# Between two layers of a graph and mixture-of-experts stack: row statistics, turning and head products tile by tile, residual products postponed, maxima two heads ahead instead of three

## What is computed

```
x = x + graph_conv(layernorm(x))                 # layer 0
x = x + attention_and_experts(layernorm(x))      # layer 0, 8 experts, 2 per row, and a shared one
x = x + graph_attention(layernorm(x))            # layer 1, 12 heads of 64   <- the change is in front of it and in it
x = x + experts(layernorm(x))                    # layer 1, 8 experts, 2 per row
```

```
ft = hh @ W_fc.T ;  a1 = ft . attn_l ;  a2 = ft . attn_r
e = leaky_relu(a1[src] + a2[dst], 0.2) ;  m = segment_max(e, dst)
alpha = exp(e - m[dst]) / segment_sum(...)
out = relu(hh @ W_res.T + segment_sum(alpha * ft[src]))
```

## Time and profile before

| | |
|---|---|
| time, median of 3 runs | 1669.37 us (1667.52 to 1672.15) |
| the profiled execution | 1672.59 us, of which the span of the trace is 1670.9 us |
| TensorE busy | 1500.3 us (90%) |
| VectorE busy | 1276.2 us (76%) |
| ScalarE busy | 854.8 us (51%) |
| GpSimd busy | 332.7 us (20%) |
| mean granted TensorE clock | 0.941 of full speed |

### The profile page before, as it was taken

One profiled execution on the slowest core, in us unless ns is written; L12 is line 12 of the kernel. 1 busy time (PEld: TensorE's weight loads), 2 busy tenths in 40 slices (PEclk: granted clock), 3 DMA queues, 4 the chain that ended last, 5 costly groups with the idle time before them and its releaser, 6 DMA issues. The chain is left out here.

```text
span 1670.9 us, 36622 instructions
## 1 busy us (share of the span) xinstructions
PE 1500.3 (90%) x14493; PEld 1277.6 (76%) x14493; DVE 1276.2 (76%) x2205; ACT 854.8 (51%) x1215; POOL 332.7 (20%) x254
## 2 busy tenths in 40 slices
PE   7987877887899999999999669966899999999997
PEld 5664445665567899999998534436899999999995
DVE  8998376775566688888888578857788888888786
ACT  1112116775544567777675125444566666666651
POOL 0004004655030000000004036655330000000040
PEclk9998898999899999999999769886999999999999
DMA  7640000000465678888886001113978888888884
GB/s 202 157 107 0 0 1 10 1 1 17 164 206 178 234 271 291 307 301 295 299 298 194 1 24 31 32 53 106 358 254 294 290 300 293 293 300 287 294 271 109
DMA packets 55554, 297.59 MB, mean 178 GB/s; under 512 B 14063, under 2 KB 14319, under 8 KB 32433
## 3 DMA queue, kind: packets, MB, share of 16 engines
q1 hardware_dynamic: 41761, 263.23, 46.0%
q0 software_dynamic: 13712, 33.26, 7.3%
HBM read 264.07 MB, written 32.34 MB: 177 GB/s over the span
## 5 line engine op out<-in xcount | busy, mean ns | idle before, releaser
L717 PE MATMUL ps<-big,wh 128*128 128x176 f16 x2160 | 497.4, 240 | 5.5 <-DVE wl L572 3.5
L721 PE MATMUL ps<-big,wl 128*128 128x176 f16 x2160 | 497.5, 239 | 0.0
L719 PE MATMUL ps<-big,wh 128*128 128x176 f16 x2160 | 497.4, 239 | 0.0
L738 PE MATMUL ps<-big,wh 128*128 128x176 f16 x2160 | 263.8, 239 | 3.0 <-DVE big L606 2.9
L738 PE MATMUL ps<-big,wl 128*128 128x176 f16 x1080 | 249.6, 240 | 0.0
L572 DVE SCALAR_TENSOR_TENSOR wl<-ext,wh 128x2304 f16<-128x2304 f32 x90 | 229.6, 2551 | 1.1 <-issue 0.9
L572 DVE SCALAR_TENSOR_TENSOR wl<-raw,wh 128x2304 f16<-128x2304 f32 x90 | 229.5, 2550 | 0.0
L493 ACT ACTIVATE wh<-raw 128x2304 f16<-128x2304 f32 x90 | 190.4, 2117 | 62.7 <-PE ps L738 51.6
L493 ACT ACTIVATE wh<-ext 128x2304 f16<-128x2304 f32 x90 | 190.5, 2117 | 51.3 <-PE ps L738 35.4
L717 PEld LDWEIGHTS ps<-big,wh 128*128 128x128 f16 x2160 | 209.2, 97 | 9.1 <-issue 3.4
L719 PEld LDWEIGHTS ps<-big,wh 128*128 128x128 f16 x2160 | 211.7, 98 | 0.2
(11 more groups left out here) (345 smaller groups left out, 2837.8 us busy)
## 6 DMA issues: line engine op xcount, KB each, us to landing
raw<-in_units SPq DMA_DIRECT2D x54, 1152.0 KB, 5.3
ext<-in_units SPq DMA_DIRECT2D x54, 1152.0 KB, 5.6
raw<-in_units SPq DMA_DIRECT2D x36, 1153.0 KB, 5.9
ext<-in_units SPq DMA_DIRECT2D x36, 1153.0 KB, 6.3
raw<-in_units_s SPq DMA_DIRECT2D x16, 769.0 KB, 4.5
ext<-in_units_s SPq DMA_DIRECT2D x16, 769.0 KB, 4.6
x_slots<-raw SPq DMA_DIRECT2D x1, 8976.0 KB
big<-x_slots POOLq DMA_DIRECT2D x17, 528.0 KB, 8.5
```

The lines of the kernel that those rows point to most:

```text
L717: nc.tensor.matmul(o, wh[:, u % RING, w_], x_, start=c == 0 and m == 0, stop=False, skip_group_check=True)
L719: nc.tensor.matmul(o, wh[:, u % RING, w_], xTl[:, c, 0:ph.n], start=False, stop=False, skip_group_check=True)
L721: ins = nc.tensor.matmul(o, wl[:, u % RING, w_], x_, start=False, stop=c == KC - 1, skip_group_check=True)
L738: ins = nc.tensor.matmul(o, l_[:, u % RING, w_], r_, start=first and k == 0 and c % 2 == 0, stop=last and k == 2, skip_group_check=True)
```

## The change

- The fence between the layers goes. VectorE's statistics are made tile by tile between the last adds: statistics of tiles 0 and 1, last add of tile 2, statistics of 2, last add of 3, statistics of 3, one square root for tiles 0 to 3 (on ScalarE ahead of the copies that fold the head weights), last add of 4, normalisation of 0 to 3; then statistics, root and normalisation of tile 4.
- TensorE turns tile by tile (6 blocks of one tile into banks 2, 3 or 0, 1), ScalarE alone copies the turned tiles to SBUF, and TensorE makes the head products of a tile (`head_values`, 6 of 132 columns, banks 4 to 7, each waiting for its tile's copy) in alternation with the turning of later tiles.
- The residual products are made apart, one tile at a time in banks 4 and 5 (`residual`, 6 of 128 columns, each waiting for the copy of the one before), among the steps of heads 0 and 1; ScalarE copies them in between.
- The maxima run two heads ahead instead of three: two heads before the loop, head h+2 in iteration h.
- `shifts_transposed(h+2)` moves in TensorE's stream from behind chunk 4 of head h-1 to between chunks 2 and 3 of head h. `shift_out(h+2)` moves in ScalarE's stream from behind exp 0 to behind exp 3, ahead of `head_out(h-1)`.
- In the last pass of layer 1's experts `gathered(1, 1)` is done one unit earlier. Copies of a1 and a2 are one instruction instead of two. The small work on gates and branches comes after a1's copy.

```diff
@@ scalar
-            fence(act, F_LAYER0)
-            root()
-            transposed_out()
+            root_part(4, NT)
             for t in range(NT):
-                act.wait_ge(s_ft, t + 1)
-                at = (4 * (t % 2) + 2) * BANK
-                nc.scalar.activation(z[:, t, :], ps[0:P, at:at + D], ACT.Copy).then_inc(s_fta, 1)
+                act.wait_ge(s_zT, t + 1)
+                nc.scalar.activation(tD[:, :, t * P:(t + 1) * P], z_turned(t), ACT.Copy).then_inc(s_zTa, 1)
+            def residual_out(t):
+                act.wait_ge(s_res, t + 1)
+                nc.scalar.activation(z[:, t, :], bank(4, 2)[0:P, 0:D], ACT.Copy).then_inc(s_fta, 1)
...
+            residual_out(0)
+            residual_out(1)
             shift_out(0)
+            residual_out(2)
+            residual_out(3)
             shift_out(1)
+            residual_out(4)
             for h in range(H):
                 for t in range(NT):
                     edge_exp(h, t)
-                    if t == 0:
-                        if h:
-                            sums_out(h - 1)
-                        if h + 2 < H:
-                            shift_out(h + 2)
+                    if t == 0 and h:
+                        sums_out(h - 1)
+                    if t == 3 and h + 2 < H:
+                        shift_out(h + 2)
                     if t == 3 and h:
                         head_out(h - 1)
@@ vector
+            dve.wait_ge(s_add, 2)
+            row_stats(0)
+            row_stats(1)
+            last_added(0, 2)
+            dve.wait_ge(s_add, 3)
+            row_stats(2)
+            last_added(0, 3)
+            dve.wait_ge(s_add, 4)
+            step(row_stats(3))
+            roots_asked(0, 4)
+            last_added(0, 4)
+            roots_of(0, 4)
             dve.wait_ge(s_add, NT)
-            fence(dve, F_LAYER0)
-            layernorm()
...
+            step(row_stats(4))
+            roots_asked(4, NT)
+            roots_of(4, NT)
...
-            for h in range(3):
+            for h in range(2):
                 for t in range(NT):
                     edge_top(h, t)
                 shifts(h)
             for h in range(H):
                 for t in range(NT):
                     edge_power(h, t)
-                if h + 3 < H:
+                if h + 2 < H:
                     for t in range(NT):
-                        edge_top(h + 3, t)
+                        edge_top(h + 2, t)
                         if t == 1 and h:
                             sums_inverted(h - 1)
-                    shifts(h + 3)
+                    shifts(h + 2)
@@ tensor
+            def z_transposed(t):
+                pe.wait_ge(s_zt, t + 1)
+                if t == 1:
+                    pe.wait_ge(s_add, NT)
                 if t >= 2:
+                    pe.wait_ge(s_zTa, t - 1)
+                for c in range(KC):
+                    ins = nc.tensor.transpose(z_turned(t)[:, c, :], z[:, t, c * 128:(c + 1) * 128], ident[0:P, 0:P])
+                ins.then_inc(s_zT, 1)
...
+            z_transposed(0)
+            z_transposed(1)
+            pe.wait_ge(s_fold, 6)
+            for t in range(NT):
+                head_values(t)
+                if t + 2 < NT:
+                    z_transposed(t + 2)
...
+            pe.wait_ge(s_a12, 1)
             source_row(0)
+            residual(0)
+            residual(1)
             shifts_transposed(0)
             source_row(1)
             flat_rows(0)
+            residual(2)
+            residual(3)
             shifts_transposed(1)
-            source_row(2)
+            residual(4)
+            pe.wait_ge(s_fta, NT)
             for h in range(H):
-                if h + 3 < H:
-                    source_row(h + 3)
+                if h + 2 < H:
+                    source_row(h + 2)
                 if h:
                     head_chunk(h - 1, 4)
-                if h + 2 < H:
-                    shifts_transposed(h + 2)
-                if h:
                     head_back(h - 1)
                 head_chunk(h, 0)
                 if h + 1 < H:
                     flat_rows(h + 1)
                 for t in range(1, 4):
                     head_chunk(h, t)
+                    if t == 2 and h + 2 < H:
+                        shifts_transposed(h + 2)
```

More of the change, by code:

```diff
@@ L46 @@
 C_ZERO, C_ALL = 2, 14
-F_GRAPH, F_MHA, F_LAYER0 = range(1, 4)
-R_Z0, R_HS, R_Z1 = range(1, 4)
+F_GRAPH, F_MHA = range(1, 3)
+R_Z0, R_HS = range(1, 3)
 def f16_pair(v):
@@ L609, in vector_steps, with ffn_vector @@
             return low, x_low, hidden
-        def ffn_vector(dve, ph, steps, at_last, step):
+        def ffn_vector(dve, ph, steps, at_last, step, adds):
             low, x_low, hidden = steps
             layer = 0 if ph is ph_0 else 1
-            sums = layer * 2 * NT
+            gathered, last_added = adds
             def one_pass(i, last):
@@ L632, in one_pass @@
                         gathered(layer, 0)
+                    if u == ph.ic - 2 and last and layer == 1:
+                        gathered(layer, 1)
                 dve.wait_ge(ph.down, ph.base + (i + 1) * ph.ic + RING)
@@ L659, in placed_last @@
                     ins.then_inc(s_lastpl, 1)
[L661 to L678, removed]
             with dve.Fori(0, at_last) as i:
@@ L682, in ffn_vector @@
             one_pass(at_last, True)
-            gathered(layer, 1)
+            if layer == 0:
+                gathered(layer, 1)
             dve.wait_ge(ph.yt, at_last * 3 + 5)
@@ L1306, in root_of @@
                 step(nc.vector.tensor_tensor(dst_, dst_, rs[:, 2, :], ALU.mult))
[L1308 to L1314, removed]
-                    ins = nc.vector.bn_aggr(mv[:, t, :], st[:, t, 0:2, :].rearrange("p a b -> p (a b)"))
-                step(ins)
-                nc.vector.tensor_scalar(rs[:, 0, :], mv[:, :, 1], 1e-5, None, ALU.add).then_inc(s_var, 1)
-                root_of(rs[:, 3, :])
-                for t in range(NT):
-                    ins = nc.vector.tensor_scalar(z[:, t, :], xres[:, t, :], mv[:, t, 0:1], rs[:, 3, t:t + 1],
-                                                  ALU.subtract, ALU.mult)
-                step(ins)
             def mean_squares(eps):
@@ L1689, in table, with gathered, last_added @@
                 nc.vector.tensor_copy(tabi[:, 0, :], tab1[:, 1, :]).then_inc(s_tab, 1)
+            def gathered(layer, a):
+                tiles = ((0, 1), (2,), (3,), (4,))[a]
+                for k in range(2):
+                    for t in tiles:
+                        if k == 0:
+                            dve.wait_ge(s_gat[t], 32 * (layer + 1))
+                        else:
+                            dve.wait_ge(s_sum, layer * 2 * NT + 2 * tiles[0] + 1 + t - tiles[0])
+                        nc.vector.scalar_tensor_tensor(out=xres[:, t, :], in0=rows[t][k], scalar=wts[:, k, t:t + 1],
+                                                       in1=xres[:, t, :], op0=ALU.mult, op1=ALU.add)\
+                            .then_inc(s_sum, 1)
+            def last_added(layer, t):
+                dve.wait_ge(s_sum, layer * 2 * NT + 2 * (t + 1 if t else 2))
+                dve.wait_ge(s_lastmm, layer * NT + t + 1)
+                nc.vector.tensor_tensor(xres[:, t, :], xres[:, t, :], last_sum(t), ALU.add).then_inc(s_add, 1)
             def shared_low(j):
@@ L1927, in _ @@
             dve.wait_ge(s_tab, 2)
-            ffn_vector(dve, ph_1, e1, last_pass(dve), step)
+            ffn_vector(dve, ph_1, e1, last_pass(dve), step, (gathered, last_added))
+            for t in range(2, NT):
+                last_added(1, t)
         @block.tensor
```

93 lines of the change are left out of this document (55 added, 38 removed).

## The result

The changed kernel takes 1703.1 us (median of 4, 1695.6 to 1710.3) against 1670.8 us (median of 4) for the kernel before on the same chip: a ratio of 1.019, 95% interval 1.0138 to 1.0243. It is slower, by 1.4 to 2.4%. The profiled execution has a span of 1702.9 us, against 1670.9 before.

A forecast was written before the change was run, and what follows sets the result against it. It saw some 60 us of one engine at a time before the loop, then a 10.15 us chain through GpSimd and ScalarE per head. -8 + 37.5 + 0 = +29.5 gave 1702, 1699 against the median; 8-in-10 range 1657 to 1711.

The forecast's parts named there:

- The source row of head 0 14 us earlier: Between the layers: tile-by-tile work brings head 0's source row to about 949.7 us against 963.86.
- The first chunk 13.6 us earlier at half clock, 20 at full: Before the loop: head 0's first chunk at 973.9 or 967.3 us against 987.52; half clock was taken.
- The table load: ScalarE before the first exp: 1.28 us by the rows; the skill's drain would make it 1.4 us later.
- `head_out(0)` 8 us earlier: End of the first head in the loop: 995 us against 1003.21, bounds 1 and 18 us earlier.
- The ring: Loop: `shift_out` ahead of `head_out` closes a chain through TensorE once a head, 11.94 us at full clock, 17.7 at half.
- 16.3 us per head, 37.5 us for eight spacings: Loop, `head_out(0)` to `head_out(8)`: 4.7 us per head over 11.61, clock falling in nearly every head; ends 2.6 and 49.
- Clock towards 0.65: Sign in the loop: TensorE's mean clock goes down from 0.84 towards 0.65.
- GpSimd idle over 4 us: Sign in the loop: GpSimd waits over 4 us ahead of `head_added` instead of 1.95.
- The tail 0, bounds -2.5 and +3: Last two heads: no `shift_out`, so they keep the old chain and change by 0 us.
- rival 4: Loop all at half clock, spacing 17.7 us, front gains only 1: 1717 us, chance 0.04.
- Rival 3: Loop: waiting for `shift_out` hardly bites, spacing stays 10.2 to 11.6 us: 1654 us; chance 0.19 together with rival 2.
- Rivals 1 and 2: Loop clock: 1, falls about as often as before, 1676 us, chance 0.24; 2, stays full, 1654, 0.19 with rival 3.

The follow-up runs named there:

- e3: The changed kernel with `head_added` moved behind mask 4 on GpSimd: 1658.9 us, one run.
- e10: The changed kernel with three added products of 128 columns per head on TensorE, between chunk 4 and the turning back: 1665.5 us.
- e6: The front of the kernel before with the changed kernel's loop over heads: 1705.7 us, 1.025 of the kernel before.
- e5: The changed kernel with eight added products of 128 columns per head on TensorE, between source row and chunk 4, heads 1 to 10: 1662.9 us.
- e4_filler: The changed kernel with eight added products of 128 columns per head on TensorE, between source row and chunk 4: 3945.5 us, one run.

## Why the prediction came out as it did

The direction, the place and the mechanism were right: 1699 us predicted against the median, 1703.1 measured.

- **The source row of head 0 14 us earlier**: 15.28, counted from the last gathered add. TensorE done with head products near 947: 950.6, of which 4.9 are the later start of the whole stretch.
- **The first chunk 13.6 us earlier at half clock, 20 at full**: 13.35 in the changed kernel, at half clock; 19.6 in e3 and e10, where the clock was full from the second residual product on. Both ends of the estimate were seen. Of the 15.3 us that the source row gains, 13.4 are left at the first chunk. The third head of maxima, which the change moves out of this stretch, is worth 7.5 alone (in e6 the first chunk comes 58.24 after the add, before 65.76). So behind the same two heads of maxima the whole new front is worth 5.8 us (58.24 less 52.41) in the changed kernel, where the residual products wait 0.7 to 0.9 us for the single pair of banks and four of five take 2.92 us at half clock. At full clock it is worth 12.1 (58.24 less the 46.12 of e10).
- **The table load**: by the rows 1.28 us. In the changed kernel it stands at 976.91 and the first exp at 978.20, 1.29 apart, so here too nothing but the load itself stands between them. The root's load, which stood in the way before at 933.72, now starts at 922.74, and ScalarE's root starts 0.20 us behind the request at 932.82.
- **`head_out(0)` 8 us earlier**: 12.6 counted from the add, 7.65 by the clock on the wall. The first head took 16.5 us where the prediction allowed 21. This step was 4.6 us too careful, and the later start of the stretch hid it.
- **The ring, 11.94 us at full clock**: 11.88, measured in e5.
- **The ring, 17.7 us with TensorE's part at half clock**: the changed kernel alternates between about 16.7 and 17.5.
- **16.3 us per head, 37.5 us for eight spacings**: 17.09 and 43.8. This is the mis-sized term, by 6.3 us. The prediction let the clock rise in the run of chunks 1 to 3, so that "chunks 1 and 2, which the chain needs, are mostly over", and let a few heads escape. The trace shows chunks 1 and 2 at half clock (4.10 to 4.43 us), the rise only behind them, and no head that escapes.
- **Clock towards 0.65**: 0.65. **GpSimd idle over 4 us**: 8.8 to 10.4 in the eight heads. The prediction had the sign right and did not give the size, which is the slack of GpSimd in a period of 17.
- **The tail 0, bounds -2.5 and +3**: +0.80.

The sum of the steps, -8 + 37.5, had two errors of opposite sign: the loop was 6.3 worse, the front 4.6 better. The hit within 4 us owes something to that luck. By the loop alone rival 4's 17.7 us per head was nearer to the 17.09 than the forecast's 16.3; its 1717 us failed on the front, which it let gain only 1 us. Rival 3 has fallen by the 6.6 to 8.0 us for which ScalarE waits for the turning of the shifts.

The rule of the Trainium skill ("TensorE: Matmul & The Clock Gate", HAM oscillation) that a hole which recurs in every iteration takes the clock down in every iteration agrees with the changed kernel's eight heads, and e5 turned it round: with the hole filled the clock was 1.00. The page tells it of a kernel whose waits were for DMA and about 3 to 5 us long; here a wait of about 2 us with one of 0.78 was enough. Rivals 1 and 2 were about this clock. Rival 2's loop at 11.94 is what e5 measured, though its 1654 us is not: e5 took 1662.9, and its front ran at half clock (25.59 us from source row to chunk).

**What stays open.** Why the last gathered add ends at one of two times (918.8 to 919.6, or 924.2 to 926.7) in kernels that are alike up to there; the kernel before, at 921.76, lies between. And why the -4.93 us behind the last head cancels it in the changed kernel; e6, whose add ended early, has the same 542 us behind `head_out(11)`. And why the same code between source row and first chunk ran at half clock in the changed kernel and e5 and at full clock in e3 and e10, which is 6.8 us of luck in any comparison of single profiles here.

## What to carry to other kernels

Put an instruction that other engines wait for (here `head_out`) ahead of one that only serves a later iteration (here the copy of the shifts), above all if the second waits for an engine that itself hangs on the first: two such lines in the wrong order cost about 50 us of 1650. Price a ring at both clocks, and ask of each hole that it leaves in TensorE whether the clock survives it; if not, the ring's price is that of half clock. A cheap test of whether a loop pays for its work or for its clock is to give TensorE more work in the hole: if that makes the kernel faster, it was the clock.

## What the runs showed of the hardware

- Added work made a kernel faster: eight products per head, 2.05 us each time, took 40 us off (1703.1 to 1662.9).
- A shorter filler that left the hole of about 2 us open still raised the clock from 0.65 to 0.88 and took 32.9 us off the eight spacings.
- The period at a clock that falls in every head repeats closely: the eight spacings of the changed kernel and of e6_loop_only, two kernels with different fronts, agree within 0.03 us each (16.82, 17.39, 16.66, 17.54 against 16.85, 17.41, 16.65, 17.55).
- One execution (e4_filler) had TensorE at about half speed, 442 against 240 ns per product in the mean of one group of 2160, and 1224 against 2793 products in the first 500 us, while the recorded clock was 1.00; the next run of the same kernel was normal.
